# Gathering and summing in a recurrent mixture of experts: twelve units beside the page pairs instead of ten

## What is computed

```
xn = layernorm(x)
s  = attn(xn)      # gated linear recurrence h = tanh(h @ A.T + u_t), then out * gate + xn
scores = sigmoid(xn @ gate_w.T);  idx = top_k(scores + gate_b, 4)
w  = scores[idx] / sum(scores[idx]) * 2.5
y  = sum over the 4 chosen experts e of w_e * (silu(xn @ g_e.T) * (xn @ u_e.T)) @ w2_e.T   # 16 experts
y  = y + shared expert(xn)
out = x + s * silu(y)
```

## Time and profile before

| | |
|---|---|
| median of 3 runs | 519.35 us |
| the 3 runs | 519.85, 519.35, 514.77 us |
| span of the profiled execution, first to last instruction | 513.9 us |
| mean granted TensorE clock of it | 0.837 |
| DMA traffic of it | 109.27 MB, 213 GB/s over the span |

### The profile page before, as it was taken

How to read it: one execution, slowest core, us unless ns; L and a number is a source line. 1 busy time by engine, 2 the same in 40 slices (tenths; PEclk the granted TensorE clock), 3 DMA queues, 4 the chain that set the end, 5 groups by cost and what they waited for, 6 DMA issues and landing times.

```text
span 513.9 us, 10001 instructions
## 1 busy us (share of the span) xinstructions
PE 339.1 (66%) x3107; PEld 261.7 (51%) x3107; DVE 311.1 (61%) x977; ACT 251.0 (49%) x462; POOL 265.4 (52%) x278
## 2 busy tenths in 40 slices
PE   0365566849467786976799968797876968645210
PEld 0352443626355665755698846575654756433100
DVE  4899776676703545545643626786776555346745
ACT  1851666536434455443787746565664644422000
POOL 2005377766646566655600165766555554436773
PEclk9976698797876889888999989999997898676555
DMA  7998499425443566654779768899977777436653
GB/s 247 305 328 281 129 343 331 161 86 201 143 165 127 175 186 201 196 172 156 216 220 269 227 192 268 281 282 285 285 243 211 249 217 225 128 119 194 174 160 126
DMA packets 88675, 109.27 MB, mean 213 GB/s; under 512 B 9649, under 2 KB 78002, under 8 KB 88626
## 3 DMA queue, kind: packets, MB, share of 16 engines
q1 hardware_dynamic: 74656, 74.47, 45.7%
q0 software_dynamic: 12288, 33.57, 20.7%
q10 hardware_dynamic: 1682, 0.59, 0.4%
HBM read 55.91 MB, written 52.69 MB: 211 GB/s over the span
## 4 chain that ended last, share of the span: by engine, by line
PE 35%; another core or an unknown queue 12%; issue 10%; ACT 8%; DVE 6%; POOL 5%; DMA 1%; ACTq 1%; POOLq 0%; DVEq 0%
PE bank L850 13%; PE bank L872 8%; PE bank L656 6%; POOL xn_parts L638 5%; PE bank L863 3%; ACT xn_f L1851 3%; PE bank L898 2%; ACT sh_h L1868 1%; ACT y_ring L1875 1%; ACT xn_f L1859 1%; ACT x_ring L1881 1%; PE bank L948 1%; DVE mix_sb L1371 1%; PE bank L774 1%
## 5 line engine op out<-in xcount | busy, mean ns | idle before, releaser
L638 POOL DMA_INDIRECT xn_parts<-y_slots,slot_u x128 | 127.2, 994 | 126.2 <-PE bank L656 39.6
L619 POOL DMA_INDIRECT x_slots<-xn_parts,slot_u x128 | 131.7, 1029 | 115.1 <-DVE slot_u L1253 36.0
L850 PE MATMUL bank<-w_all,xn_f 128*128 (+1 forms) x864 | 122.2, 295 | 22.2 <-issue 11.5
L850 PEld LDWEIGHTS bank<-w_all,xn_f 128*128 128x128 f16 x864 | 87.3, 106 | 44.8 <-issue 30.6
L1524 DVE SCALAR_TENSOR_TENSOR xn_f<-bank,xn_f 128x256 f32<-128x256 f32 x72 | 30.5, 424 | 111.9 <-ACT xn_f L1859 69.3
L1851 ACT ACTIVATE xn_f<-bank 128x1024 f16<-128x1024 f16 x72 | 73.5, 1022 | 36.7 <-remote 22.3
L872 PE MATMUL bank<-w_all,sh_silu 128*128 (+1 forms) x432 | 68.2, 299 | 5.5 <-ACT y_ring L1875 4.2
L1875 ACT ACTIVATE y_ring<-bank 128x512 f32<-128x512 f32 x72 | 42.9, 596 | 54.4 <-PE bank L872 33.7
L1859 ACT ACTIVATE xn_f<-bank 128x256 f32<-128x256 f32 x72 | 27.5, 382 | 55.0 <-remote 32.4
L656 PE MATMUL bank<-ident_h,w_stage 128*128 128x128 f16 x576 | 48.6, 231 | 1.5 <-issue 1.4
L872 PEld LDWEIGHTS bank<-w_all,sh_silu 128*128 128x128 f16 x432 | 41.8, 106 | 14.5 <-issue 7.5
(11 more groups left out here) (215 smaller groups left out, 456.9 us busy)
## 6 DMA issues: line engine op xcount, KB each, us to landing
w_stage<-x_slots SPq DMA_DIRECT2D x72, 256.0 KB
y_slots<-y_ring SPq DMA_DIRECT2D x72, 256.0 KB
x_slots<-zero_h SPq DMA_DIRECT2D x10, 1024.0 KB
x_ring<-in_x SPq DMA_DIRECT2D x32, 256.0 KB
w_stage<-in_w13t SPq DMA_DIRECT2D x17, 256.0 KB
x_ring<-in_x SPq DMA_DIRECT2D x8, 512.0 KB, 7.7
out<-mix_sb SPq DMA_DIRECT2D x15, 256.0 KB
w_stage<-in_w2t SPq DMA_DIRECT2D x17, 128.0 KB
```

Of the source, the lines that this page charges most:

```text
L619: eng.indirect_dma_start(out=x_slots, out_offset=bass.IndirectOffsetOnAxis(ap=slot_u[:, n * TOPK + k:n * TOPK + k + 1], axis=0), in_=xn_pa ...
L638: eng.indirect_dma_start(out=fin_y[:, r, j, k, :], out_offset=None, in_=y_slots[0:2 * READY_PAIR[c] * P, :], in_offset=bass.IndirectOffset ...
L850: mm = eng.matmul(gu[:, j * 2 * F:(j + 1) * 2 * F], xg_T[:, n % 2, ((j * 2 + px) * KD + k) * P:((j * 2 + px) * KD + k + 1) * P], weights_o ...
```

## The change

One line, the list of iterations at which units stand beside the pairs:

```diff
@@ -369,7 +369,7 @@
         SHIFT = {21: 0, 48: 1}
         OUT_SLOT = 43
         CHECK, FALLBACK, PARTS = 50, 54, 55
-        UNIT_PAIR = tuple(40 + 10 * c // 3 for c in range(10))
+        UNIT_PAIR = tuple(40 + 3 * c for c in range(12))
         STATES_SLOT = 86
         RANK_SLOT = {6: 4, 21: 5, 36: 6}
         EXPERT_SLOT = {17: 1, 46: 2}
```

## The result

The kernel before takes 517.75 us in the median of 4 runs (514.77 to 519.85), the changed kernel 500.15 us in the median of 4 (498.38 to 500.95). The profiled execution took 500.95 us with a span of 499.1, against 513.9 before.

The account below looks back on a forecast made before the run. POOL's gathers, one behind the other, were taken to bound the end: -10.4 us there plus 2.4 for the pairs gave -8.0 on a span of 513.9, so 511.4 us against the median of 519.35; range 505 to 519.

Parts of the forecast that it names:

- POOL is what bounds the end: End of the kernel: it runs through gathers on POOL one behind the other, 32 of them in 42.5 us.
- -10.4 us: End: unit 12's eight gathers move into the loop, leaving 24 and removing the stretch from 464.97 to 475.37 us.
- What the pairs pay: 2.4 us: Loop: added unit work costs the pairs 1.5 us on PE and 0.9 us on DMA, together 2.4 us.
- the lower bound of -2: Loop: pairs may get 2 us faster, as gathers no longer bunching behind a late `product` may clear the queues.
- The idle stretch of 5.87 us: ACT in iteration 70: idle 5.87 us until 457.80, without a releaser; part of POOL's 8.85 us of idle time.
- 5.4 us between the span and the device time: Whole kernel: the median of 519.35 us was taken as 5.4 above the span of 513.9 us.
- the ring come free at iterations 63.3, 66.3 and 69.3: Loop, kernel before: the ring of three buffers came free late, so POOL fell behind its timetable.
- The costs of the parts: Loop: PE 1.5 us, DMA 0.9 us, DVE and ACT costed at nothing; 2.4 us together.
- POOL has no hole to fill: Rival, loop's end: without POOL's idle time the gain is 4.4 us minus 2.4, so 517.4 us; chance 0.2.
- The pairs pay the full price: Rival, loop: added units cost 6.2 us each, 12.4 for two against 10.4 gained, so 521.4 us; chance 0.12.
- unit 14 waits for DVE: Rival, end: unit 11's `product` comes after a late unit 12, POOL idles 3 us, so 514.4 us; chance 0.13.
- VectorE's lock on GpSimd: Gathers beside DVE: VectorE in a two-port mode blocks descriptor writes; even 3.8 us would fall into POOL's idle time.

Follow-up runs that it names:

- hold12: Changed kernel with unit 12's gathers also waiting for unit 10's `product`, so 32 gathers are left for the end: 500.28 us, 0.970; repeated in another comparison, 500.73 us, 0.969.
- run 6: Not a run label: "run" is a verb here, in "the last pairs then run 6 to 9 us faster".
- after_side: The changed kernel unaltered, run again in another comparison: 499.33 us, 0.967 of the kernel before.
- plain12: Changed kernel with unit 12's eight blocks loaded by plain SP transfers from fixed pages instead of POOL gathers, same bytes: 497.71 us, 0.952 of the kernel before.
- long condition: The runs of this study beside which the kernel before took 516 to 524 us; the prediction, its trace and the main result belong to it.
- hold7to11: Changed kernel with first gathers of units 7 to 11 held by waits to the pairs that released them in the kernel before: 515.52 us, 0.997.
- short condition: The last six runs of this study, beside which the kernel before took 443 us.
- after_short: Changed kernel, fourth, sixth and eighth gathers of units 11 and 12 waiting for the landing of a gather two back: 448.43 us, 1.013 of the kernel before.
- nopace_again: Changed kernel without half-pair waits for units 7 and up: 441.80 us, 0.996 in the short condition; as nopace in the long condition, 529.58 us, 1.014.
- short11_pace12: Changed kernel, unit 11's gathers waiting for landings two back, unit 12's last six for second products of pairs 68 to 70: 446.29 us, 1.007.
- before_cut: Kernel before, with the third, fifth and seventh gathers of units 7 to 11 waiting until the two before them landed: 530.80 us, 1.028.
- after_cut: Changed kernel, with the third, fifth and seventh gathers of units 11 and 12 waiting until the two before them landed: 508.22 us, 0.986.
- pace12: Changed kernel with unit 12's last six gathers waiting two by two for the second products of pairs 68 to 70: 503.96 us, 0.963 of the kernel before.
- before_again: The kernel before, unaltered, profiled again in the short condition: 443.20 us, 1.000.

## Why the prediction was wrong

**"POOL is what bounds the end" and "-10.4 us".** In the timeline this happened to the letter: unit 12 in the loop, 24 gathers in a row, the stretch from pair 71 to the last gather 10.2 us shorter. As a term of the sum it isn't safe, though. hold12 puts the eight gathers back to the end and costs nothing, because the last pairs then run 6 to 9 us faster. I had costed unit 12's gathers beside the last pairs at nothing, since DMA stood at 0.72, then 0.45 and 0.37. They cost about what they saved, and after_side with hold12_side says the same. DMA's share was the wrong thing to go by, as plain12 shows: the same bytes there, issued elsewhere, leave the pairs fast.

**"What the pairs pay: 2.4 us" is the step that failed.** In the long condition it was -8.3, in size and sign, beyond the lower bound of -2. I had named the right mechanism at that bound, "gathers that no longer bunch behind a late `product`", and gave it a number without a row. There were rows for it: POOL idle for 4.78, 6.26 and 8.85 us in front of units 10 to 12, each followed by its unit without a pause, with the pairs at their slowest beside them. hold7to11 shows it: with only those starts put back, pairs go from 142.85 to 156.37 us, 13.5 more and so more than the whole gain, and the kernel from 500.43 to 515.52. The forecast took its direction from the 10.4 us at the end, which hold12 shows to be worth nothing once the pairs are counted too. That it said "faster" at all was in that sense luck.

**The idle stretch of 5.87 us** I took as a thing to place, not as one of a kind. In the whole trace of the kernel before such stretches on ACT sum up to 90 us:

```profile
ACT xn_f L1859 <- remote: 32.4, 14, 5.9
...
ACT xn_f L1851 <- remote: 22.3, 19, 3.1
...
ACT y_ring L1875 <- remote: 19.0, 9, 3.6
...
ACT scores L1766 <- remote: 16.4, 4, 5.6
```

(in total, times, longest). It is more idle time of ACT than any releaser with a name explains, and all of it is waiting for PE's signals.

**Two smaller slips.** The prediction put 5.4 us between the span and the device time, the span of one execution against the median of others. In every run whose span is on record the time is 1.7 to 2.0 us above it. The span came out at 499.1 for 505.9, 6.8 us off, and the slip added 3.6 to that. It also has the ring come free at iterations 63.3, 66.3 and 69.3 in the kernel before; by the old list these `multiply` steps stand at 62.3, 65.3 and 68.3. Nothing in the sum used them.

**The costs of the parts** can be read in the short condition, where such stretches are absent: there the pairs take 112.06 us for 109.37, +2.7, against my +2.4. This is one execution each and within the 3.2 us by which executions of one kernel differed above, so it supports the size but doesn't prove it. after_short, nopace_again and short11_pace12, which have the same list of units, have 111.95 to 112.46.

**The rivals.** "POOL has no hole to fill" (517.4 us, a ratio of 0.996) is what happens in the short condition, at 0.997, by the mechanism that I named, an unbroken row on POOL, though it begins with unit 0. That the size agrees too is luck: I had still given the change 4.4 us of that row. In the long condition it was wrong. "The pairs pay the full price" was wrong in both, and "unit 14 waits for DVE" too: POOL goes into unit 14 at 471.04 after a gap of 0.30 us.

**VectorE's lock on GpSimd.** I left the rule of the Trainium skill ("SBUF — State Buffer", section "SBUF: two separate sides") out of the sum. It speaks of VectorE in a two-port mode, and no row here says in which mode an operation of DVE ran, so the runs can't test it. What they show is how gathers fare beside a denser DVE. In the short condition DVE is busy for 27.31 of 32 us from 340 to 372:

```profile
L638 POOL DMA_INDIRECT xn_parts<-y_slots,slot_u x128: 942/948/2601, 263.8 to 434.2; - x128
...
340.00:372.00 32.00, 29.38 (x317) 25.22 (x313) 27.31 (x68) 24.20 (x45) 24.62 (x24) 1.00 1.00 326
```

Most gathers are at the floor, 942 ns at the shortest and 948 in the median. But 43 of the 128 last over 1.05 us, where it is 21 in the long condition, and the mean is 1039 ns for 994. So more of them are held up beside the denser work, by 5.8 us in all; by what isn't shown.

**What stays open.** Why PE's signals come late in the long condition isn't shown, nor how the gathers' timing acts on them. I can't say either that the gain passes through these stretches alone: on ACT from 290 to 470 us they sum up to 53.5 us in the kernel before and to 59.9 in the changed one, while its pairs are 8 us faster; before_cut has 30.9 and after_cut 40.5. Over the whole trace they aren't concentrated in rows either: 59 of the 90 us lie beside gathers or scatters that follow each other within 0.6 us, and these cover 320.9 of the 513.9 us, nearly the same share. Shown are three things. In the long condition the timing of the gathers alone moves the pairs by over 20 us (135.82 in pace12, 162.59 in nopace, timed side by side). In the short condition no timing tried made them faster, and cuts in units 7 to 11 made them 7.7 us slower. And PE's late signals come with the long condition alone.

## What to carry to other kernels

When a queue of gathers waits for a buffer, price the lateness twice: the hole in front, and the row without a pause behind it, beside which the other engines of this kernel ran slower in one of its two conditions; an earlier release can be worth more beside the loop than at the end. Before a term is priced, sum up the idle time whose releaser the trace doesn't name, on every engine, and find out which semaphore ended it: where it is a sixth of the span, as on ACT here, the gain of a change in order belongs to that condition, and the same change may be worth 3% today and nothing tomorrow. And hold a moved piece of work back in its old place by one wait: hold12 said in one run that the term I was surest of bought nothing.

## What the hardware showed that I had not expected

- **One program, two times that far apart**: 443 and 517 us, a factor of 1.17, without a change to it. PE's clock is 0.889 of full speed in the profiled execution of the one and 0.837 of the other, and PE's busy time 307.0 and 339.1 us. Stretches that end with a late signal of PE stand on ACT (90 us), POOL (38) and DVE (16) in the long condition and nowhere in the short one:

```profile
ACT xn_parts L1887 <- DVE xn_parts L1575: 40.0, 14, 9.7
ACT xn_f L1859 <- PE bank L850: 35.7, 58, 4.4
ACT y_ring L1875 <- PE bank L872: 29.4, 71, 4.9
```

  These are the first lines of ACT's waits in before_again, and each of its releasers has a name.
- **Gathers have a floor that load doesn't move**: 0.95 us and a gap of 0.30 us, beside DMA engines at 1.00 of their time and 326 GB/s as at half of that. The kernel's time in the short condition follows from it: 128 x 1.34 = 171.7 us from the first gather on, and 6.5 us behind the last. The 1.34 is the mean, with the longer ones in it.
- **The same transfers are harmless from another queue**: plain12 moves unit 12's bytes through SP beside the last pairs, and these take 135 us as in the runs in which those bytes aren't moved there at all (hold12, 134).
